# Two stack loads moved behind the band copies in SyncE's step of the first attention

## The chip, the cores and the metric

The kernel runs on one core of one Trainium2 chip. A core has TensorE (PE in the profile, with PEld for its weight loads), VectorE (DVE), ScalarE (ACT), GpSimd (POOL) and SyncE (SP), which work beside each other and wait for each other through semaphores. All DMAs of this program are issued by SyncE, on one queue that 16 DMA engines serve. The metric is the device time of one execution in microseconds (us), lower is better.

## The reference, cut to what matters

The program is a block of two layers on x of 8 x 512 x 128 (batches, positions T, channels C): attention, layer norm, feed-forward, layer norm, and the same again with another attention and another feed-forward. The change touches only the first attention, which has 16 heads of 8 channels and scores with two relative-position terms:

```
rel = arange(t)[None, :] - arange(t)[:, None]
rel_pos = clip(rel + 64, 0, 127);  p2c_pos = clip(-rel + 64, 0, 127)
scores = einsum('bhqd,bhkd->bhqk', Q, K) * scale
c2p = einsum('bhqd,shd->bhqs', Q, pos_key) * scale      # then gathered at rel_pos
p2c = einsum('bhkd,shd->bhks', K, pos_query) * scale    # then gathered at p2c_pos, transposed
probs = softmax(scores + c2p + p2c, axis=-1)
ctx = einsum('bhqk,bhkd->bhqd', probs, V);  out = ctx @ Wo.T + bo
```

## The kernel before

Five stages follow each other: an opening that projects queries, keys and values, the first attention (`attention(0)`), a stage between the layers, the second attention (`attention(1)`) and a dense stage. Both attentions are made by one function; what holds for the first alone stands under `if rel`.

The first attention goes through 128 heads (8 batches by 16), one after the other, in four row tiles of 128 each. One pass is called a step. Each engine has its own list of steps: 4 steps written out (`FIRST`), a hardware loop of 8 steps a turn, and the rest written out. In step n the engines are at different heads:

- PE multiplies score tiles six tiles ahead of head n (`score_tile`), turns the probabilities of head n, weighs the values of the group before (`weigh`), forms the key side of head n+7 (`key_side`, L741) between the turn of tile 1 and that of tile 2, and the correction of head n+5 (`correction`, L748 and L749) at the step's end. Its order is fixed: an instruction that waits holds all behind it.
- DVE puts in the far side of a tile (`mix`, L936), adds the band (`finish`, L948), takes the row maximum (`row_max`, L956) and copies the key side out (`key_out`, L755).
- ACT takes exponentials (L1046), copies turned probabilities (L1053) and, last in its step, the correction of head n+5 (`corr_out`, L761).
- SP, in step n (`sync_step`, L675), issues the DMAs by which position terms are sheared through memory and by which later heads' data come in. "Stack" is the tile `a_stks`, which holds a head's queries and keys, split in bf16 parts.

What SP issues in step n, before the change, in this order:

| piece | line | head | waits for | KB |
|---|---|---|---|---|
| key-side write, `shear_a_write` | L634 | n+6 | DVE copied the key side | 256 |
| two stack loads, `head_load` | L608, L609 | n+8 | PE finished the score tiles of head n | 96 and 48 |
| correction write, `shear_b_write` | L646 | n+4 | DVE added the band of head n, ACT copied the correction | 256 |
| band read, `shear_b_read` | L652 | n+3 | the correction write of head n+3 landed | 512 |
| table and offset loads (every fourth step) | L621, L628, L629 | a group of 4 | nothing | 96 and 48 |
| skewed read, `shear_a_read` | L640 | n+6 | the key-side write of this step landed | 256 |
| group store and values load (every fourth step) | L671, L673 | a group of 4 | ACT copied the group's output | 256 and 72 |

A stack load of head n+8 goes into the slot of head n; PE reads it first in `key_side` of its step n+1. The band read of head n+3 is awaited by DVE before `finish` of that head, also in its step n+1. The skewed read of head n+6 is awaited by PE before `correction` of that head, at the end of its step n+1. The four steps after which a group is complete are called a group here, and its fourth step, which issues the table, offset, store and values DMAs too, the long step.

The two stack loads are these lines:

```
sp.dma_start(stk[j][0:SR, KS:QLO + 1, :], rows).then_inc(stk_in[j], 16)
sp.dma_start(stk[j][0:SR, QHI, :], rows[:, 1, :]).then_inc(stk_in[j], 16)
```

`hold(q, event, value)` makes the queue wait until a semaphore has reached a value, and counts the wait.

Of the kernel before, what the change touches and what calls it, by code (L numbers as in the profile page):

```python
# [50 lines left out]
CORR_AHEAD, KEY_AHEAD, LOAD_AHEAD = 5, 7, 8  # L51
# [13 lines left out]
def build(nc, t):  # L65

    top = ExitStack()
    with top:
# [430 lines left out]
        def attention(layer):  # L499
# [9 lines left out]
            def s(name):  # L509
                return sem(f"a{layer}_{name}")  # L510
# [30 lines left out]
            score_mm, fixed, added, maxed, exped = (s(n) for n in ("score_mm", "fixed", "added", "maxed", "exped"))  # L541
# [53 lines left out]
            def hold(q, event, value):  # L595

                q.wait_ge(event, BASE + value)
                q.sem_inc(held_off, 1)
# [3 lines left out]
            def head_load(sp, h):  # L602

                j, b = h.slot, h.n // H
                own = bass.ts(h.n % H, DH)
                if rel:
                    rows = stack[0][b, :, own].rearrange("a c j t -> (c j) a t")
                    sp.dma_start(stk[j][0:SR, KS:QLO + 1, :], rows).then_inc(stk_in[j], 16)  # L608
                    sp.dma_start(stk[j][0:SR, QHI, :], rows[:, 1, :]).then_inc(stk_in[j], 16)  # L609
                else:  # L610
                    src = stack[1][b, own].rearrange("c j w -> (c j) w")
                    spins = src[:, 3 * T:5 * T + 2].rearrange("r (a t) -> r a t", a=2)[:, :, 0:T]
                    sp.dma_start(stk[j][0:SR, KEY:NEAR + 1, :].rearrange("r a t -> r (a t)"), src[:, 0:3 * T]).then_inc(stk_in[j], 16)
                    sp.dma_start(stk[j][0:SR, FAR, :], src[:, 2 * T:3 * T]).then_inc(stk_in[j], 16)
                    sp.dma_start(stk[j][SR:R1, EDGE, :], src[:, T + 1:2 * T + 1]).then_inc(stk_in[j], 16)
                    sp.dma_start(stk[j][SR:R1, NEAR:FAR + 1, :], spins).then_inc(stk_in[j], 16)

            def tab_load(sp, h):

                src = table[bass.ds(h.n % H, GROUP)].rearrange("h r c -> r h c")  # L620
                sp.dma_start(tabs[0:SR, h.slot:h.slot + GROUP, :], src).then_inc(tab_in[h.slot // GROUP], 16)  # L621

            def offset_load(sp, h):

                src, own = offsets[h.n // H, bass.ds(h.n % H, GROUP)], slice(h.slot, h.slot + GROUP)
                event = offset_in[h.slot // GROUP]
                for arr in (QLO, QHI):
                    sp.dma_start(stks[RA:RB, own, arr, :], src[:, arr - QLO].rearrange("h k t -> k h t")).then_inc(event, 16)  # L628
                sp.dma_start(stks[RB:RS, own, KS, :], src[:, 2:4].rearrange("h a k t -> (a k) h t")).then_inc(event, 16)  # L629

            def shear_a_write(sp, h):

                hold(sp, key_copied, h.n + 1)
                sp.dma_start(shear_a[h.slot % 4, :, SPAN:SPAN + T], keyside[h.slot % 4][:, :]).then_inc(a_written[h.slot % 4], 16)  # L634

            def shear_a_read(sp, h):

                hold(sp, a_written[h.slot % 4], 16 * (h.use(4) + 1))
                skew = bass.AP(shear_a.tensor, (h.slot % 4) * 128 * PITCH_A, [[PITCH_A + 1, 128], [1, T]])
                sp.dma_start(sheared[h.slot % 4][:, :], skew).then_inc(sheared_in[h.slot % 4], 16)  # L640

            def shear_b_write(sp, h):

                hold(sp, corr_copied, h.n + 1)
                dst = shear_b[h.slot % 4, :, REL:PITCH_B].rearrange("p (n c) -> p n c", n=NT)[:, :, 0:REL]
                sp.dma_start(dst, corr[h.slot % 2][:, :, :]).then_inc(b_written[h.slot % 4], 16)  # L646

            def shear_b_read(sp, h):

                hold(sp, b_written[h.slot % 4], 16 * (h.use(4) + 1))  # L650
                skew = bass.AP(shear_b.tensor, (h.slot % 4) * 128 * PITCH_B + REL, [[PITCH_B - 1, 128], [1, NT * wide]])
                sp.dma_start(band[h.slot % bands][:, :, :].rearrange("p n c -> p (n c)"), skew).then_inc(band_in[h.slot % bands], 16)  # L652

            def edge_write(sp, h):

                hold(sp, corr_copied, h.n + 1)
                dst = shear_e[h.slot % E_RING].rearrange("(n p) c -> p n c", p=128)[:, :, REL:2 * REL]
                sp.dma_start(dst, corr[h.slot % corrs][:, :, :]).then_inc(e_written[h.slot % corrs], 16)

            def edge_read(sp, h):  # L660

                hold(sp, e_written[h.slot % corrs], 16 * (h.use(corrs) + 1))
                skew = bass.AP(shear_e.tensor, (h.slot % E_RING) * T * PITCH_E + REL,
                               [[PITCH_E - 1, 128], [128 * PITCH_E, NT], [1, REL]])
                sp.dma_start(band[h.slot % bands][:, :, :], skew).then_inc(band_in[h.slot % bands], 16)

            def group_store(sp, h, more):

                g = h.use(GROUP)
                hold(sp, out_copied, g + 1)  # L670
                sp.dma_start(heads_out[bass.ts(g, GROUP)], outs[:, :]).then_inc(out_written, 16)  # L671
                if more:
                    sp.dma_start(vs[h.slot // GROUP][:, 0:GROUP * NT * VC], values[g + vslots]).then_inc(v_in[h.slot // GROUP], 16)  # L673

            def sync_step(sp, i, j, left, weighed=True):  # L675

                n = unroll * i + j
                if rel:
                    if left >= CORR_AHEAD + 1:
                        shear_a_write(sp, Head(i, j + CORR_AHEAD + 1))  # L680
                    if left >= LOAD_AHEAD:
                        hold(sp, score_mm, 4 * (n + 1))
                        head_load(sp, Head(i, j + LOAD_AHEAD))
                    if left >= CORR_AHEAD - 1:
                        hold(sp, added, 4 * (n + 1))
                        shear_b_write(sp, Head(i, j + CORR_AHEAD - 1))
                    if left >= CORR_AHEAD - 2:
                        shear_b_read(sp, Head(i, j + CORR_AHEAD - 2))
                    if j % GROUP == GROUP - 1 and left >= LOAD_AHEAD + GROUP:
                        tab_load(sp, Head(i, j + LOAD_AHEAD + 1))  # L690
                    if j % GROUP == GROUP - 1 and left >= LOAD_AHEAD:
                        offset_load(sp, Head(i, j + LOAD_AHEAD + 1 - GROUP))
                    if left >= CORR_AHEAD + 1:
                        shear_a_read(sp, Head(i, j + CORR_AHEAD + 1))
                else:
                    if left >= CORR_AHEAD:
                        edge_write(sp, Head(i, j + CORR_AHEAD))
                    if weighed and left >= CORR_AHEAD - 1 or 0 < j < FIRST and not weighed:
                        if weighed:
                            hold(sp, added, 4 * (n + CORR_AHEAD - bands))  # L700
                        edge_read(sp, Head(i, j + CORR_AHEAD - 1))
                    if left >= LOAD_AHEAD:
                        if not isinstance(i, int) or n + LOAD_AHEAD >= unroll:
                            hold(sp, maxed, 4 * (n + LOAD_AHEAD - unroll + 1))
                        head_load(sp, Head(i, j + LOAD_AHEAD))
                if weighed and j % GROUP == GROUP - 1:
                    group_store(sp, Head(i, j + 1 - 2 * GROUP), left >= GROUP * (vslots - 1))
# [1416 lines left out]
```

## Time and profile before

| | us |
|---|---|
| median of 3 runs | 1885.64 (1884.05 to 1885.77) |
| the profiled execution's own time | 1885.77 |
| its span, first to last instruction | 1883.3 |
| PE busy | 1703.0 (90%) |
| DVE busy | 1461.2 (78%) |
| ACT busy | 1448.3 (77%) |

The page of the profile cuts the span into 40 slices of 47.1 us and gives the busy share of each in tenths:

```profile
## 2 busy tenths in 40 slices
PE   4469999999999999868758999999999989999998
DVE  5659999999999999859887999999999872443332
ACT  4449999999999999858888999999999972322222
PEclk9669999999999999989879999999999989999999
DMA  6779999999999999766998777777777751010000
```

The first attention is the stretch of 9s that begins in the third slice and ends in the seventeenth, from about 116 us to 780 us. There PE, DVE, ACT and the DMA engines are all nearly full. The second attention has 7s in the DMA row, and the dense stage at the end hardly uses DMA. Two more parts of the page name what the change moves: the chain that ended last, and the DMAs with the time from issue to landing.

```profile
## 4 chain that ended last, share of the span: by engine, by line
PE 45%; DMA 19%; SPq 10%; issue 10%; DVE 6%; ACT 6%; POOL 0%; DVEq 0%; ACTq 0%; POOLq 0%
DMA shear_a<-a_keyside 13%; PE bank L1936 12%; PE bank L842 11%; PE bank L855 7%; DMA a_band<-shear_e 5%; PE bank L821 4%; DVE a_negmax L956 2%; ACT a_probt L1053 2%; PE bank L823 2%; PE bank L1928 1%; PE bank L1929 1%; PE bank L1957 1%; ACT a_prob L1046 1%; PE bank L741 1%; PE bank L748 1%
...
## 6 DMA issues: line engine op xcount, KB each, us to landing
a_band<-shear_b SPq DMA_DIRECT2D x128, 512.0 KB, 5.5
shear_a<-a_keyside SPq DMA_DIRECT2D x128, 256.0 KB, 4.2
a_sheared<-shear_a SPq DMA_DIRECT2D x128, 256.0 KB, 4.0
shear_b<-a_corr SPq DMA_DIRECT2D x128, 256.0 KB, 3.4
```

### The profile page before, as it was taken

Reading aid. Unit: us, or ns where it says so; the run is one execution under the profiler, and the core shown is the slowest. Engines: PE = TensorE matmul, PEld = TensorE weight load, DVE = VectorE, ACT = ScalarE, POOL = GpSimd, SP = SyncE. Lnnn points to the kernel's source line nnn. Section 1 sums busy time; section 2 is a strip of 40 time slices with the busy share of each in tenths; the row PEclk is TensorE's granted clock in tenths of the full one; section 3 lists DMA queues with packets and bytes.
Section 4 is the critical chain, followed back from the end, with each engine's and each line's share of the span. In section 5 each row is a group of like instructions: output and inputs, shape, how many; then the busy total and the mean of one; then the engine's idle time right before and its main releaser. Section 6 shows DMA issues by size and latency. Waiting matters only on the chain.

```text
span 1883.3 us, 45550 instructions
## 1 busy us (share of the span) xinstructions
PE 1703.0 (90%) x12438; PEld 1047.7 (56%) x12438; DVE 1461.2 (78%) x3533; ACT 1448.3 (77%) x2573; POOL 80.1 (4%) x102
## 2 busy tenths in 40 slices
PE   4469999999999999868758999999999989999998
PEld 2146666666666666545535666666666544455453
DVE  5659999999999999859887999999999872443332
ACT  4449999999999999858888999999999972322222
POOL 0000000000000000015410000000000000000000
PEclk9669999999999999989879999999999989999999
DMA  6779999999999999766998777777777751010000
GB/s 200 275 244 282 291 302 297 295 286 288 279 296 291 286 289 292 239 192 207 350 329 250 218 219 225 220 220 219 221 224 218 219 156 44 28 39 22 22 6 11
DMA packets 414360, 404.45 MB, mean 215 GB/s; under 512 B 36969, under 2 KB 334561, under 8 KB 414177
## 3 DMA queue, kind: packets, MB, share of 16 engines
q1 hardware_dynamic: 414305, 403.80, 69.4%
q8 instruction: 24, 0.39, 0.1%
q14 instruction: 31, 0.25, 0.0%
HBM read 226.89 MB, written 176.30 MB: 214 GB/s over the span
## 4 chain that ended last, share of the span: by engine, by line
PE 45%; DMA 19%; SPq 10%; issue 10%; DVE 6%; ACT 6%; POOL 0%; DVEq 0%; ACTq 0%; POOLq 0%
DMA shear_a<-a_keyside 13%; PE bank L1936 12%; PE bank L842 11%; PE bank L855 7%; DMA a_band<-shear_e 5%; PE bank L821 4%; DVE a_negmax L956 2%; ACT a_probt L1053 2%; PE bank L823 2%; PE bank L1928 1%; PE bank L1929 1%; PE bank L1957 1%; ACT a_prob L1046 1%; PE bank L741 1%; PE bank L748 1%
## 5 line engine op out<-in xcount | busy, mean ns | idle before, releaser
L1046 ACT ACTIVATE a_prob<-bank,a_negmax 128x512 f32<-128x512 f32 x1024 | 697.4, 735 | 50.3 <-DVE a_negmax L956 47.8
L956 DVE TENSOR_REDUCE a_negmax<-bank 128x1 f32<-128x512 f32 x1024 | 698.5, 682 | 0.1
L842 PE MATMUL bank<-ident,a_prob 128*128 128x128 f32 x4096 | 597.6, 279 | 18.9 <-ACT a_probt L1053 15.2
L1053 ACT COPY a_probt<-bank 128x512 f32<-128x512 f32 x1024 | 586.7, 629 | 20.5 <-PE bank L842 20.0
L842 PEld LDWEIGHTS bank<-ident,a_prob 128*128 128x128 f32 x4096 | 446.4, 142 | 85.4 <-issue 49.4
L948 DVE TENSOR_TENSOR bank<-bank,a_band 128x128 f32<-128x128 f32 (+3 forms) x1024 | 349.0, 341 | 56.5 <-DMA a_band<-shear_e 23.0
L821 PE MATMUL bank<-a_stks 74*128 74x192 bf16 (+7 forms) x1024 | 325.3, 318 | 29.3 <-ACT a_prob L1046 25.4
L855 PE MATMUL bank<-a_probt,a_vs 128*32 128x256 f32 (+1 forms) x2792 | 294.6, 495 | 0.4 <-ACT a_probt L1053 0.4
L821 PEld LDWEIGHTS bank<-a_stks 74*128 74x128 bf16 (+1 forms) x1024 | 100.2, 98 | 204.9 <-ACT a_prob L1046 182.3
L823 PE MATMUL bank<-a_stks 74*128 74x320 bf16 (+5 forms) x768 | 201.7, 263 | 0.0
L936 DVE COPY_PREDICATED bank<-a_mask,bank 128x128 f32<-128x128 uint32 (+1 forms) x512 | 139.4, 272 | 27.7 <-PE bank L827 26.6
L2002 DVE TENSOR_TENSOR d_drop<-bank,d_s 128x128 f32<-128x128 f32 x32 | 7.1, 282 | 170.4 <-PE bank L1957 170.4
L748 PE MATMUL bank<-ident,a_sheared 128*128 128x128 f32 x512 | 106.6, 286 | 29.8 <-DMA a_sheared<-shear_a 22.0
L755 DVE COPY a_keyside<-bank 128x512 f32<-128x512 f32 x128 | 87.8, 686 | 39.4 <-PE bank L741 39.2
L827 PE MATMUL bank<-a_stks 74*128 74x128 bf16 (+1 forms) x512 | 109.7, 214 | 7.9 <-DVE bank L936 6.8
L1936 PE MATMUL bank<-d_ha,d_h1T 128*128 128x512 f32 x256 | 112.3, 592 | 0.0
L1936 PE MATMUL bank<-d_hb,d_h2T 128*128 128x512 f32 x256 | 111.2, 592 | 0.0
L761 ACT COPY a_corr<-bank 128x512 f32<-128x512 f32 x128 | 75.9, 593 | 40.2 <-PE bank L749 25.4
L748 PEld LDWEIGHTS bank<-ident,a_sheared 128*128 128x128 f32 x512 | 74.9, 146 | 43.2 <-issue 24.5
L749 PE MATMUL bank<-a_tabs,a_stks 65*128 65x128 bf16 x512 | 98.4, 226 | 0.0
L855 PEld LDWEIGHTS bank<-a_probt,a_vs 128*32 128x32 f32 x2792 | 56.2, 108 | 67.9 <-issue 67.8
L1987 ACT ACTIVATE d_hb<-bank,d_fs 128x512 f32<-128x512 f32 x32 | 22.0, 687 | 90.6 <-PE bank L1936 90.6
(179 smaller groups left out, 1600.5 us busy)
## 6 DMA issues: line engine op xcount, KB each, us to landing
a_band<-shear_b SPq DMA_DIRECT2D x128, 512.0 KB, 5.5
shear_a<-a_keyside SPq DMA_DIRECT2D x128, 256.0 KB, 4.2
a_sheared<-shear_a SPq DMA_DIRECT2D x128, 256.0 KB, 4.0
shear_b<-a_corr SPq DMA_DIRECT2D x128, 256.0 KB, 3.4
shear_e<-a_corr SPq DMA_DIRECT2D x128, 256.0 KB, 2.3
a_band<-shear_e SPq DMA_DIRECT2D x128, 256.0 KB, 3.2
a_stks<-stack SPq DMA_DIRECT2D x256, 96.0 KB, 2.5
a_stks<-stack SPq DMA_DIRECT2D x384, 48.0 KB, 2.4
```

Of the source, the lines that this page charges most:

```text
L748: pe.matmul(corr_bank[:, q], sheared[h.slot % 4][:, q], ident[:, :], is_transpose=True, start=True, stop=False)
L821: last = pe.matmul(score[:, 0:c], k[:, qlo, q], k[:, keys, 0:c], start=True, stop=True)
L823: last = pe.matmul(score[:, c:T], k[:, qhi, q], k[:, keys, c:T], start=True, stop=True)
L827: last = pe.matmul(other[:, 0:e - a], k[:, qhi, q], k[:, keys, a:e], start=True, stop=True)
L842: last = pe.transpose(turned_bank[k][:, n * 128:(n + 1) * 128], prob[h.slot % 2][:, n, k * 128:(k + 1) * 128], ident[:, :])
L855: part = pe.matmul(cbank[32 * j:32 * j + VW, cols], vs[g][:, at:at + VW], probt[h.slot + j][:, k, cols], start=(k == 0), stop=(k == NT - 1 ...
L936: v.copy_predicated(score[:, a:e], mask[:, 0:e - a], other[:, 0:e - a]).then_inc(fixed, 1)
L948: v.tensor_tensor(score[:, a:e], score[:, a:e], band[h.slot % bands][:, n, w:w + e - a], ALU.add).then_inc(added, 1)
L956: v.tensor_reduce(negmax[h.slot % 2][:, n:n + 1], score[:, :], AX.X, ALU.max, negate=True).then_inc(maxed, 1)
L1046: nc.scalar.activation(prob[h.slot % 2][:, n, :], score[:, :], ACT.Exp, bias=negmax[h.slot % 2][:, n:n + 1]).then_inc(exped, 1)
L1053: nc.scalar.copy(probt[h.slot][:, k, :], turned_bank[k][:, :]).then_inc(copied, 1)
L1936: last = pe.matmul(dst[:, :], w[:, k, 128 * m:128 * m + 128], src[:, k, :], start=(k == 0), stop=(k == KH - 1))
```

## The change

In SP's step of the first attention the two stack loads of head n+8 move from behind the key-side write to behind the band read. The wait ahead of them is now for the row maxima of head n instead of its score tiles. Nothing else changes; the other four engines' instructions are the same.

```
                     if left >= CORR_AHEAD + 1:
                         shear_a_write(sp, Head(i, j + CORR_AHEAD + 1))
-                    if left >= LOAD_AHEAD:
-                        hold(sp, score_mm, 4 * (n + 1))
-                        head_load(sp, Head(i, j + LOAD_AHEAD))
                     if left >= CORR_AHEAD - 1:
                         hold(sp, added, 4 * (n + 1))
                         shear_b_write(sp, Head(i, j + CORR_AHEAD - 1))
                     if left >= CORR_AHEAD - 2:
                         shear_b_read(sp, Head(i, j + CORR_AHEAD - 2))
+                    if left >= LOAD_AHEAD:
+                        hold(sp, maxed, 4 * (n + 1))
+                        head_load(sp, Head(i, j + LOAD_AHEAD))
```

On SP's queue an ordinary step of the first attention reads so (L634 key-side write, L608 and L609 stack loads, L646 correction write, L652 band read, L640 skewed read; - is before, + is the change, names carry the buffer's number):

```order
 L634 DMA shear_a<-a_keyside_76 128x512
-L608 DMA a_stks<-stack 48x2x512
-L609 DMA a_stks<-stack 48x512
 L646 DMA shear_b<-a_corr_67 128x4x128
 L652 DMA a_band_68<-shear_b 128x1024
+L608 DMA a_stks<-stack 48x2x512
+L609 DMA a_stks<-stack 48x512
 L640 DMA a_sheared_80<-shear_a 128x512
```

The correction write and the band read now follow the key-side write at once, and the stack loads stand between the band read and the skewed read.

In the long step of a group, on the same queue, the table and offset loads (L621, L628) follow:

```order
 L634 DMA shear_a<-a_keyside_74 128x512
-L608 DMA a_stks<-stack 48x2x512
-L609 DMA a_stks<-stack 48x512
 L646 DMA shear_b<-a_corr_67 128x4x128
 L652 DMA a_band_70<-shear_b 128x1024
+L608 DMA a_stks<-stack 48x2x512
+L609 DMA a_stks<-stack 48x512
 L621 DMA a_tabs<-table 48x4x256
 L628 DMA a_stks<-offsets 3x4x512 x2
```

Here the stack loads stand between the band read and the table load.

## Rows read from the trace of the kernel before

**Rows 1.** The page, part 1: busy us (share of the span) and instructions by engine.

```profile
PE 1703.0 (90%) x12438; PEld 1047.7 (56%) x12438; DVE 1461.2 (78%) x3533; ACT 1448.3 (77%) x2573; POOL 80.1 (4%) x102
```

**Rows 2.** Windows view: stretch, its us, busy us (count) per engine, clock, DMA share.

```profile
200.00:400.00 200.00, 196.53 (x1872) 131.74 (x1871) 189.01 (x487) 189.26 (x346) 0.00 (x0) 1.00 0.94 294
```

**Rows 3.** Waits of SP's queue, 126 to 780 us: in total, times, longest us.

```profile
SPq L598 <- DMA shear_a<-a_keyside: 99.4, 88, 3.6
SPq L598 <- ACT a_corr L761: 11.5, 18, 2.1
SPq L598 <- DVE a_keyside L755: 4.2, 7, 1.1
```

**Rows 4.** Timeline of SP's queue, steps 47 and 48: start us, us.

```profile
372.73 0.32 SPq L634 DMA_DIRECT2D shear_a<-a_keyside  x1
...
375.31 0.39 SPq L646 DMA_DIRECT2D shear_b<-a_corr  x1
375.81 0.44 SPq L652 DMA_DIRECT2D a_band<-shear_b  x1
376.51 0.34 SPq L621 DMA_DIRECT2D a_tabs<-table  x1
...
380.38 0.33 SPq L634 DMA_DIRECT2D shear_a<-a_keyside  x1
...
381.75 0.35 SPq L609 DMA_DIRECT2D a_stks<-stack  x1
382.29 0.39 SPq L646 DMA_DIRECT2D shear_b<-a_corr  x1
382.79 0.44 SPq L652 DMA_DIRECT2D a_band<-shear_b  x1
```

**Rows 5.** DMA view, 375.7 to 376.7 us: count, KB, us to landing.

```profile
a_band<-shear_b SPq DMA_DIRECT2D x1, 512.0 KB, 5.1
...
a_tabs<-table SPq DMA_DIRECT2D x1, 96.0 KB, 4.6
```

**Rows 6.** DMA view, 382.7 to 383.2 us, the band read of step 48.

```profile
a_band<-shear_b SPq DMA_DIRECT2D x1, 512.0 KB, 5.3
```

**Rows 7.** DMA view, 126 to 780 us, medians of the two stack loads.

```profile
a_stks<-stack SPq DMA_DIRECT2D x119, 96.0 KB, 3.0
...
a_stks<-stack SPq DMA_DIRECT2D x119, 48.0 KB, 3.3
```

**Rows 8.** Timeline of PE, key sides of heads 13, 53, 56, 61, 69, 72, 125.

```profile
156.82 0.39 PE L741 MATMUL bank<-a_stks,a_tabs 65*128 65x512 bf16 x1
...
371.40 0.39 PE L741 MATMUL bank<-a_stks,a_tabs 65*128 65x512 bf16 x1
...
387.60 0.39 PE L741 MATMUL bank<-a_stks,a_tabs 65*128 65x512 bf16 x1
...
414.28 0.39 PE L741 MATMUL bank<-a_stks,a_tabs 65*128 65x512 bf16 x1
...
458.14 0.39 PE L741 MATMUL bank<-a_stks,a_tabs 65*128 65x512 bf16 x1
...
474.34 0.39 PE L741 MATMUL bank<-a_stks,a_tabs 65*128 65x512 bf16 x1
...
764.18 0.39 PE L741 MATMUL bank<-a_stks,a_tabs 65*128 65x512 bf16 x1
```

**Rows 9.** Timeline of SP's queue, steps 63 and 64.

```profile
460.00 0.32 SPq L634 DMA_DIRECT2D shear_a<-a_keyside  x1
...
468.10 0.33 SPq L634 DMA_DIRECT2D shear_a<-a_keyside  x1
...
470.51 0.44 SPq L652 DMA_DIRECT2D a_band<-shear_b  x1
```

**Rows 10.** DMA view, 470.4 to 470.8 us, the band read of step 64.

```profile
a_band<-shear_b SPq DMA_DIRECT2D x1, 512.0 KB, 6.4
```

**Rows 11.** DMA view, 361.9 to 362.2 us, the band read of step 44.

```profile
a_band<-shear_b SPq DMA_DIRECT2D x1, 512.0 KB, 3.9
```

More of the change, by code:

```diff
@@ L680, in sync_step @@
                         shear_a_write(sp, Head(i, j + CORR_AHEAD + 1))
-                    if left >= LOAD_AHEAD:
-                        hold(sp, score_mm, 4 * (n + 1))
-                        head_load(sp, Head(i, j + LOAD_AHEAD))
                     if left >= CORR_AHEAD - 1:
@@ L688, in sync_step @@
                         shear_b_read(sp, Head(i, j + CORR_AHEAD - 2))
+                    if left >= LOAD_AHEAD:
+                        hold(sp, maxed, 4 * (n + 1))
+                        head_load(sp, Head(i, j + LOAD_AHEAD))
                     if j % GROUP == GROUP - 1 and left >= LOAD_AHEAD + GROUP:
```

## The prediction, written before the changed kernel ran

> **What bounds the kernel now.** I read the page's busy times first: PE is busy for 90% of the span [rows 1], more than any other engine. The windows view of the stretch in which the change lies, the first attention, is sharper: from 200 to 400 us PE is busy for 196.5 of 200 us at full clock, DVE and ACT for 189, and the DMA share is 0.94 [rows 2]. So PE sets the pace, and whatever makes PE stand still there is lost; but the DMA queue has hardly any room either. Eight heads take 414.28 - 371.40 = 42.88 us on PE, read from the key sides of heads 53 and 61 [rows 8], which is 5.36 a head. From head 13 to head 125 the same rows give 764.18 - 156.82 = 607.4 us for 14 such eights, where 14 x 42.88 would be 600.3. So the whole loop loses only 7 us to anything but its steady pace.
>
> Then the waits of SP's queue in that loop [rows 3]: 99.4 us, in 88 of about 120 steps, for the key-side write to land, 11.5 us for ACT's copy of the correction, and 4.2 us for DVE's copy of the key side. SP is thus a second chain (write, landing, skewed read, next write) that runs at nearly PE's pace with little slack. When a DMA that PE or DVE needs comes late, it is because this chain and the queue behind it are late.
>
> **The change, part by part.** No instruction is added or dropped. PE, DVE, ACT and POOL have the same lists.
>
> The new wait, for the maxima of head n, costs nothing in the loop. The loads now stand behind the correction write, which waits for ACT's copy of head n+4's correction; ACT makes that at the end of its step n-1, behind the exponentials of head n, and these need the maxima. So the maxima are always there first. Behind this wait stand the skewed read and the next key-side write; in the first step alone, whose correction was copied in the opening, it may hold them, once and for no more than one row maximum.
>
> The correction write and the band read go out earlier by up to the issue of two loads. In step 48 the second load starts at 381.75 and the correction write at 382.29, 0.54 later [rows 4], so the two take some 1.1 us. DVE waits for the band read hardly at all, so this can only take away part of the 7 us of loss above: between 0 and 7. I take 5, since a late band read and a late skewed read are what the loss looks like, and both get slack if PE slips for another reason.
>
> The stack loads go back in the queue, behind 256 + 512 KB. This is where the time should change. Now they land 3.0 and 3.3 us after issue [rows 7], long before PE's key side wants them. How long does a small load behind a band read take? The table load is just that: issued at 376.51 behind the band read of 375.81 [rows 4], it lands after 4.6 us, at 381.1, and the band read after 5.1, at 380.9 [rows 5]. So a load behind the band read lands 0.2 us after it. The band read itself then has 144 KB less ahead of it, so the loads should land about when the band read lands today.
>
> The Trainium skill (DMA: Bandwidth & Descriptors, section on queues, rings and completion order) says that each DMA engine takes a queue's descriptors in ring order, but that completion is not first in, first out over the engines. By the first half the loads cannot overtake, and this sum holds; by the second they might finish before the band read, and the sum would shrink towards the second rival below. The table load's landing, 0.2 us behind the band read [rows 5], speaks for the first.
>
> When does PE want them? Step 48 loads head 56, whose key side starts at 387.60 [rows 8]. The band read of step 48 is issued at 382.79 [rows 4] and lands 5.3 us later [rows 6], at 388.1: 0.5 us too late. In step 64 the band read goes at 470.51 [rows 9] and takes 6.4 [rows 10], so 476.9, where head 72's key side starts at 474.34 [rows 8]: 2.5 late. In step 44 the band read takes 3.9 [rows 11], 1.4 less than in step 48, and is not late. Only the step after a long one is late as a rule: the long step takes 380.38 - 372.73 = 7.65 us on SP [rows 4], against 5.36 on PE.
>
> Does PE pay this lateness once or again and again? If SP keeps its own times, PE slips once, and the next late load finds PE already late. But where SP has been waiting for PE (for the key side that DVE copies), SP slips along, and the next group pays again. The least distance from a key side to its write is head 53's, 371.40 [rows 8] to 372.73 [rows 4], 1.33 us. A group's price is its lateness less the distance beyond 1.33 in the long step ahead of it. Step 48: 0.5 - 0 = 0.5. Step 64: head 69's key side at 458.14 [rows 8], its write at 460.00 [rows 9], distance 1.86, so 2.5 - 0.5 = 2.0.
>
> There are 27 groups in the loop from step 12 to step 116. In 16 the band read lands as in steps 44 and 48, late and not late in turn: 8 x 0.5 = 4.0. In 11 it lands like step 64's or between; 5 are as late as step 64, 5 x 2.0 = 10.0, and for the other 6 I take a quarter of that, 6 x 0.5 = 3.0 (between 0 and 12). Together 17.0. Off this comes what the band read gains by its earlier issue where the queue had run dry: between 0 and 1.1 a priced group; I take 0.2, as the loads' own transfer comes back behind it, so 19 x 0.2 = 3.8.
>
> The long step on SP may grow: there the correction's copy is what ended the wait before the correction write in many groups, and the two loads, which were issued during that wait, now come after it, 1.1 us. The correction write to the band read and the loads then keep their times, so I cost it at nothing. Its cover is the skewed read's slack; without it the price is up to 27 x 1.1 = 30 us.
>
> Sum: 17.0 - 3.8 - 5 = +8.2 us, say +8.5 for the half microsecond by which the second load trails the first. On the profiled execution's 1885.77 (span 1883.3 and 2.5 around it) that is 1894.3; the median of the runs, 1885.64, is the same within 0.1.
>
> **The rivals.**
>
> The lateness is paid once. SP mostly waits for its own write to land (99.4 us) and rarely for the key side (4.2 us) [rows 3], so SP may keep its times when PE slips. Then PE slips by the largest lateness and no more, about 2.8 us, and this slack takes part of the 7 us away: 1885.77 + 2.8 less 0 to 3, so 1886 to 1888.6. Against it: in steps 47 and 48 SP had no slack at all towards the key side (1.33).
>
> Faster: the loads do not fall behind the band read, and the band read's earlier issue counts. The place is DVE's wait for the band and PE's wait for the skewed read between 415 and 530 us and after 690 us, where the 7 us are lost. If the loads still land within about 3.3 us of their own issue, as today [rows 7], they are in time even when issued 1.1 to 1.7 us later, and up to 7 us come back: 1879 to 1882. It decides at a load landing of some 5 us. Against it speaks the table load [rows 5].
>
> Much slower: the longer long step is not covered. SP's chain has no room to give 1.1 us in 27 groups, the next key-side writes are late, and PE waits for the corrections: +8.5 and most of 30, 1916. Against it: between the late steps SP has caught up before the next long step, since it waits there for the key side.
>
> **How the numbers follow.** Forecast (price paid again in part of the groups) 0.56, with its own range 1889 to 1903; paid once 0.20; faster 0.16; much slower 0.08. A measurement of this kernel cannot tell less than 0.2%, 3.8 us, from no change. Of the forecast's share about 0.05 lies within it, so: slower 0.51 + 0.08, with 0.01 from paid once, 0.60; same 0.24; faster 0.16. Predicted 1894.3. The range goes from 1882, the upper end of the faster case, to 1908, by which a part of the unpriced 30 us is taken in.
>
> **What would show it.** In the profile after, the stack loads' landing should be 4.5 to 5.5 us in the median in place of 3.0 and 3.3. PE's (or its weight load's) idle time before L741 should be released by the DMA of the stack, in a dozen to two dozen places, mostly in steps right after a long one, worth 10 to 20 us in all; before, no such wait is there. Eight heads should take more than 42.88 us in most eights. DVE's waits for the band and PE's for the skewed read should shrink. SP should wait less for the write's landing and more for the key side's copy. The prediction is wrong if L741 waits for no load, or if the loads land in some 3 us; its mechanism is right but its size wrong if the waits are there and come to under 5 or over 25 us.

## The result, and the profile after

| | us |
|---|---|
| before, median of 4 runs | 1885.7 (1884.05 to 1888.66) |
| changed, median of 4 runs | 1936.22 (1933.13 to 1944.24) |
| ratio | 1.0272, 95% interval 1.0239 to 1.0307 |

The change makes the kernel slower by 50.5 us. 8.5 were forecast, with 1908 as the upper end of the range. The profiled execution of the changed kernel took 1944.98 us, with a span of 1943.2; its page, from parts 1 and 2:

```profile
span 1943.2 us, 45550 instructions
...
PE 1721.4 (89%) x12438; PEld 1057.7 (54%) x12438; DVE 1463.4 (75%) x3533; ACT 1453.5 (75%) x2573; POOL 80.1 (4%) x102
...
PE   5469999999999999977667999999999989999998
DVE  5568888889888888876977899999999973344332
...
PEclk8669999999999999988978999999999989999999
DMA  6778988889888888855999777777777761001000
```

DVE and the DMA engines, at 9 in most slices of the first attention before, are mostly at 8 now: neither has become the limit. PE is busy for 18 us more though it does the same work, which already points at its clock [rows 1]. The DMA view of 126 to 834 us has the medians of the two stack loads, 3.0 and 3.3 us before [rows 7]:

```profile
a_stks<-stack SPq DMA_DIRECT2D x119, 96.0 KB, 3.4
...
a_stks<-stack SPq DMA_DIRECT2D x119, 48.0 KB, 4.3
```

The groups of instructions at the key side, 126 to 834 us (line, engine, what, busy us and mean ns, then idle time before and what ended it):

```profile
L755 DVE COPY a_keyside<-bank 128x512 f32<-128x512 f32 x121 | 83.1, 687 | 62.8 <-PE bank L741 62.6
L741 PE MATMUL bank<-a_stks,a_tabs 65*128 65x512 bf16 x121 | 47.1, 390 | 41.6 <-DMA a_stks<-stack 25.9 <-issue 13.1 <-ACT a_probt L1053 1.9
```

PE now stands for 41.6 us before its key sides, and DVE stands behind it. The trace names a stack load as what ended 25.9 us of this; for the rest it names ACT (1.9) or nothing. The landing times settle it: summed by head over heads 16 to 119, 38.0 us of the idle time stand before heads 0 mod 4, those loaded in the step after the long one, and 0.2 before all others; and before all 26 of these heads the key side starts within 0.25 us of the later load's landing. Two other waits are gone. The kernel before had these between 126 and 780 us, and the changed one has neither between 126 and 834:

```profile
DVE bank L948 <- DMA a_band<-shear_b: 2.3, 4, 0.8
PE bank L748 <- DMA a_sheared<-shear_a: 1.9, 3, 1.1
```

The waits of SP's queue in the same stretch (the changed kernel's answer to [rows 3]):

```profile
SPq L598 <- ACT a_corr L761: 119.4, 75, 3.4
SPq L598 <- DMA shear_a<-a_keyside: 43.5, 33, 2.3
SPq L598 <- DVE a_keyside L755: 2.9, 2, 2.7
```

SP used to wait mostly for its own write to land; now it waits mostly for ACT's copy of the correction, ten times as long as before. One group in detail, the same steps 63 and 64 as in [rows 9]; timeline of SP's queue (start us, us):

```profile
488.36 0.35 SPq L634 DMA_DIRECT2D shear_a<-a_keyside  x1
490.42 0.37 SPq L646 DMA_DIRECT2D shear_b<-a_corr  x1
490.91 0.43 SPq L652 DMA_DIRECT2D a_band<-shear_b  x1
491.81 0.34 SPq L608 DMA_DIRECT2D a_stks<-stack  x1
492.34 0.35 SPq L609 DMA_DIRECT2D a_stks<-stack  x1
492.94 0.32 SPq L621 DMA_DIRECT2D a_tabs<-table  x1
...
494.91 0.35 SPq L640 DMA_DIRECT2D a_sheared<-shear_a  x1
...
496.72 0.33 SPq L634 DMA_DIRECT2D shear_a<-a_keyside  x1
497.35 0.37 SPq L646 DMA_DIRECT2D shear_b<-a_corr  x1
497.84 0.58 SPq L652 DMA_DIRECT2D a_band<-shear_b  x1
498.84 0.34 SPq L608 DMA_DIRECT2D a_stks<-stack  x1
499.37 0.35 SPq L609 DMA_DIRECT2D a_stks<-stack  x1
```

The long step goes from 488.36 to 496.72, 8.36 us, where the same step took 8.10 before [rows 9] and step 47 took 7.65 [rows 4]. Single steps differ, so the means over 25 long steps count: 7.81 us before, 8.51 now. SP stood 1.7 us before the correction write; ACT's copy ended at 490.32. Before, the two loads were issued in that time; now they come behind it. In the means over the 25 steps the correction write keeps its place (2.13 us after the key-side write before, 2.10 now), and from the band read to the next key-side write it takes 5.92 us instead of 5.17. The DMA view of 498.7 to 499.6 us has the landing of step 64's two loads:

```profile
a_stks<-stack SPq DMA_DIRECT2D x1, 96.0 KB, 4.4
a_stks<-stack SPq DMA_DIRECT2D x1, 48.0 KB, 5.3
```

499.37 + 5.3 = 504.7. PE's timeline there (idle time and its releaser in brackets):

```profile
501.58 0.63 PE L842 MATMUL bank<-ident,a_prob 128*128 128x128 f32 x4
502.14 0.64 PE L855 MATMUL bank<-a_probt,a_vs 128*32 128x256 f32 x8
504.77 0.39 PE L741 MATMUL bank<-a_stks,a_tabs 65*128 65x512 bf16 x1 [1.99 <-DMA a_stks<-stack]
```

PE stands 2 us for the load that SP issued last. And then comes what no term of the prediction had. Windows of the same place (PE, PEld, DVE, ACT and POOL busy, granted clock, DMA share, GB/s):

```profile
501.60:506.20 4.60, 2.61 (x30) 1.42 (x28) 2.35 (x8) 2.67 (x6) 0.00 (x0) 1.00 1.03 348
506.20:509.60 3.40, 3.40 (x26) 2.51 (x19) 2.11 (x6) 1.72 (x4) 0.00 (x0) 0.50 0.70 205
```

After a stretch in which PE was busy for 2.61 of 4.60 us the granted clock is 0.50, 1.2 GHz, for 3.4 us, and PE is busy throughout. There are 11 stretches of 3.4 us at 1.2 GHz in the loop, 37.5 us in all; before, the loop had none and ran at 2.4 GHz. The Trainium skill (TensorE: Matmul & The Clock Gate, section on oscillation in real kernels) describes kernels whose stops for a DMA send the array back to half its clock, so that the next piece of work starts slow; this trace agrees in kind.

To compare runs I use one number from each trace beside its ratio: the group time, the mean distance between the key sides of heads 14 and 18, 18 and 22, and so on to 118, 26 groups of four heads. It was 21.67 us before and is 23.59 now: 1.92 x 26 = 50 us. That is not the whole difference of the two traces, whose spans are 59.9 us apart: 4 us more lie in the rest of the loop and 6 behind it. The profiled execution of the changed kernel was also its longest; in the others the granted clock over the span was 0.950 to 0.953, here 0.948. So the shares below are those of this trace.

The 10 groups that touch a half-clock stretch take 24.93 us, the 16 others 22.75. But PE also stood longer in the former, 1.88 us before the key side in the mean against 1.21. Among stops of nearly the same length, 1.50 to 1.78 us, five groups with a half-clock stretch take 24.68 us and three without take 23.22, so the clock costs about 1.5 us each time. A fit over all 26 says the same, and meets every group within 0.1 us: a group takes 21.57 us, plus 0.98 times PE's stop, plus 1.51 where the clock fell. Hence, of the 50 us, PE's stops are some 38 and the clock 15, and about 3 come back elsewhere.

### The profile page after: what moved, and what is told of

It is laid out like the page before. It is cut to its first block, busy times and chain, and to the rows that moved or that the text cites. A ratio compares the mean times of both kernels' runs of the same rounds, so it can differ in the third digit from the quotient of the medians.

```text
span 1943.2 us, 45550 instructions
## 1 busy us (share of the span) xinstructions
PE 1721.4 (89%) x12438; PEld 1057.7 (54%) x12438; DVE 1463.4 (75%) x3533; ACT 1453.5 (75%) x2573; POOL 80.1 (4%) x102
## 4 chain that ended last, share of the span: by engine, by line
PE 43%; SPq 16%; issue 13%; DMA 12%; DVE 8%; ACT 7%; DVEq 0%; POOL 0%; ACTq 0%; POOLq 0%
PE bank L1936 11%; PE bank L842 10%; PE bank L855 6%; DMA a_band<-shear_e 6%; DMA a_stks<-stack 4%; PE bank L821 4%; DVE a_negmax L956 3%; ACT a_probt L1053 3%; ACT a_prob L1046 2%; PE bank L823 2%; PE bank L1928 1%; PE bank L1929 1%; DVE bank L948 1%; PE bank L741 1%; PE bank L748 1%
## 5 line engine op out<-in xcount | busy, mean ns | idle before, releaser
L842 PE MATMUL bank<-ident,a_prob 128*128 128x128 f32 x4096 | 603.8, 281 | 21.8 <-ACT a_probt L1053 15.5
L842 PEld LDWEIGHTS bank<-ident,a_prob 128*128 128x128 f32 x4096 | 451.8, 143 | 89.9 <-issue 51.3
L741 PE MATMUL bank<-a_stks,a_tabs 65*128 65x512 bf16 x128 | 51.3, 400 | 58.1 <-DMA a_stks<-stack 25.9
```

Of the source, the lines that this page charges most:

```text
L842: last = pe.transpose(turned_bank[k][:, n * 128:(n + 1) * 128], prob[h.slot % 2][:, n, k * 128:(k + 1) * 128], ident[:, :])
```

## The experiments

Every run was taken beside the kernel before on its own chip. "Long step" is the mean over the 25 long steps of steps 16 to 115, key-side write to key-side write; "half clock" is the time at clock 0.50 within the loop. Group times, steps and stops come from one trace of each run. A load is called late where PE starts the key side within 0.25 us of the landing of the later of the two loads.

| run | ratio to before, interval | group us | long step us | half clock us |
|---|---|---|---|---|
| before | 1 | 21.67 | 7.81 | 0 |
| the change | 1.0272 (1.0239 to 1.0307) | 23.59 | 8.51 | 37.5 |
| order only | 1.0284 (1.0258 to 1.0309) | 23.48 | 8.53 | 37.5 |
| wait only | 1.0008 (0.9992 to 1.0024) | 21.66 | 7.65 | 0 |
| loads between write and read | 1.0020 (1.0004 to 1.0035) | 21.82 | 7.71 | 0 |
| loads behind the wait alone | 1.0096 (1.0070 to 1.0122) | 22.51 | 8.22 | 3.4 |
| changed after the long step only | 1.0027 (1.0002 to 1.0051) | 21.90 | 7.69 | 0 |
| changed in the three others | 1.0129 (1.0088 to 1.0170) | 22.80 | 8.51 | 0 |
| changed in the long step only | 1.0111 (1.0069 to 1.0153) | 22.30 | 8.10 | 0 |
| changed in the three short ones | 1.0044 (1.0026 to 1.0061) | 21.92 | 7.33 | 0 |
| change, key side later | 1.0188 (1.0139 to 1.0236) | 22.81 | 8.43 | 3.4 |
| old order, key side later | 1.0102 (1.0059 to 1.0146) | 22.34 | 7.35 | 0 |
| change, store from ACT | 1.0065 (1.0038 to 1.0091) | 22.39 | 7.21 | 0 |
| old order, store from ACT | 1.0035 (1.0017 to 1.0054) | 22.17 | 6.31 | 0 |
| change, filler on PE | 1.0220 (1.0179 to 1.0260) | 23.04 | 8.47 | 0 |
| old order, store early | 1.0023 (0.9999 to 1.0048) | 21.74 | 7.70 | 0 |

**Order only.** The change with the old wait.

```
-                        hold(sp, maxed, 4 * (n + 1))
+                        hold(sp, score_mm, 4 * (n + 1))
```

> The new order of SP's queue with the old wait (score tiles of head n) ahead of the two stack loads. Theory A (the loads land too late for PE's key side, because they stand last, behind the correction's wait, the correction write and the band read): the same as the change, ratio to before 1.022 to 1.030, heads 0 mod 4 with loads landing within 0.25 us of their key side. Theory C (the new wait for the row maxima costs): 1.00 to 1.005.

1938.09 us, the same as the change. The order is the whole of it.

**Wait only.** The old order with the new wait.

```
-                        hold(sp, score_mm, 4 * (n + 1))
+                        hold(sp, maxed, 4 * (n + 1))
```

> The old order with the new wait (row maxima of head n in place of its score tiles). The maxima come after the key side's copy on DVE, by a COPY_PREDICATED and a TENSOR_REDUCE, about 1 us, so SP may stand up to 0.6 us in steps where it had no slack. Theory A: ratio 1.000 to 1.006, loads landing well ahead of the key side (slack 2 us and more). Theory C: 1.02 or more.

1885.81 us. The wait costs nothing that can be told, even in the place where it could be last. Theory C is out.

**Loads between write and read.** `head_load` (with its wait) stands between `shear_b_write` and `shear_b_read`.

```
                         shear_b_write(sp, Head(i, j + CORR_AHEAD - 1))
+                    if left >= LOAD_AHEAD:
+                        hold(sp, maxed, 4 * (n + 1))
+                        head_load(sp, Head(i, j + LOAD_AHEAD))
                     if left >= CORR_AHEAD - 2:
                         shear_b_read(sp, Head(i, j + CORR_AHEAD - 2))
```

> Loads (with the new wait) behind the correction write, ahead of the band read. They still stand behind ACT's correction copy but not behind the 512 KB. Theory A in its queue form (the band read ahead of them is what makes them late): they land 1.5 to 2.5 us earlier than in the change, the lateness of about 1.5 us a group is mostly gone, ratio 1.000 to 1.008. Theory B (standing behind the wait for ACT's correction copy, which closes a loop through PE, is what costs): 1.018 to 1.027.

1889.19 us. Ahead of the 512 KB instead of behind them the loads land 5.0 us into the step after the long one (mean), where in the change it is 7.3, and almost all of the loss is gone. So being behind ACT's copy is not enough for the loss, against theory B.

This run also shows something that the others hide. SP issues the same things behind ACT's wait as in the change, and yet the long step does not grow (7.71 us): the copy comes 1.29 us after the key-side write, where it comes at 1.82 before and at 2.00 in the change, and the skewed read goes out at 5.70 us, before at 5.77. So issues behind the wait did not lengthen the step here: ACT's copy came sooner by about as much.

**Loads behind the wait alone.** The wait for ACT's copy is made first, then the loads, then the write.

```
+                    if left >= CORR_AHEAD - 1:
+                        hold(sp, corr_copied, n + CORR_AHEAD)
+                    if left >= LOAD_AHEAD:
+                        hold(sp, maxed, 4 * (n + 1))
+                        head_load(sp, Head(i, j + LOAD_AHEAD))
                     if left >= CORR_AHEAD - 1:
```

> Loads behind the waits of the correction write but ahead of both the write and the band read: only the wait is ahead of them, no other transfer. Theory A in its queue form: 0.998 to 1.004, slack of the loads at the key side over 1.5 us. Theory B: 1.018 to 1.027, since the wait ahead of them is that of the change. If both parts count, the ratio rises from this run over the one with the loads between to the change.

1904.5 us: slower than with the loads between write and read. Neither theory had that. No load is late here; what is late are the reads. The waits in this run, 126 to 780 us:

```profile
PE bank L750 <- DMA a_sheared<-shear_a: 19.9, 24, 1.8
DVE bank L950 <- DMA a_band<-shear_b: 11.7, 20, 1.5
```

In the long step the correction write goes out 1.7 us after ACT's copy, 0.1 in the change; the step grows to 8.22 us, and DVE and PE stand for the band and for the skewed read. This was the first run to show that the length of SP's long step can go with a loss without any late load.

**Changed after the long step only, and in the three others.** The same `if`, by the step's place in its group.

```
+ loads last where j % GROUP == 0, in the old place elsewhere      (first run)
+ loads last where j % GROUP != 0, in the old place elsewhere      (second run)
```

> The change only in every fourth step, the one after the long step; in the other three the stack loads and their wait stand as before. Before, in this step, the band read lands 7.7 us after the step's first issue and the key side starts 6.5 us after it, so the loads come 1.2 us late if they land with the band read; the long step keeps its 7.8 us. Theory D (late loads in this one step, paid by every group): ratio 1.006 to 1.018, loads of heads 0 mod 4 landing at the key side in most groups. Theory E (the long step, grown by two issues behind ACT's wait, is what costs): 0.999 to 1.004.

> The complement: the change in three steps of four, the long one among them, and the old order in the step after the long one. The loads there are early again; the long step is longer by up to 1.1 us. Theory D: 1.000 to 1.008. Theory E: 1.015 to 1.027. If the two parts stand in series on one path (the long step, then the late loads), this run and the one with the change in the fourth step alone cost clearly less together than the whole change's 51 us.

1896.3 us (beside 1891.35 for before) and 1917.12 us. In the first 24 of 106 loads are late and PE stands 10.1 us for them, and yet it costs only 0.3%, 6 us over the 26 groups: the long step keeps its length. The lower bound of 1.006 was missed, so theory D alone falls. In the second no load after the long step is late, and it costs 1.3%. That is over theory D's range and under theory E's, and the run is not clean: 49 of its 106 loads are late, for heads 1 to 3 mod 4, PE stands 15.1 us before these key sides, and in other places for the skewed read (15.9 us). Together the two runs cost 1.6%, not 2.7%: the two parts make something that neither has.

**Changed in the long step only, and in the three short ones.** The cleaner pair, by the long step itself.

```
+ loads last where j % GROUP == GROUP - 1      (first run)
+ loads last where j % GROUP != GROUP - 1      (second run)
```

> The change in the long step alone (every fourth); the other three steps keep the old order. Theory G (the growth of SP's long step behind ACT's correction copy costs about 1 us a group by itself): SP's long step 8.3 to 8.6 us against 7.8, no load late at the key side, no half clock, ratio 1.009 to 1.015. If the long step's growth were harmless by itself and only the loads' place counted: 0.999 to 1.004.

> The complement: the change in the three other steps, the old order in the long one. Theory G: the long step keeps 7.8 us; the loads of the step after it come late but SP keeps its times, so the lateness is paid about once; ratio 1.001 to 1.007, no half clock or hardly any. If the late loads are what the change costs: 1.012 or more.

1906.71 and 1895.24 us (before: 1889.01). The long step alone costs 1.1%, the short ones 0.4%, both ratios as theory G had them. Its details were not all right. In the first run the long step went to 8.10 us, less than expected, and loads are late after all, 21 of 106: those that the long step itself issues, for which PE stands 8.6 us. In the second the long step fell to 7.33 us, and PE stands 10.4 us at the key side, where it is 38.0 in the change with the same loads late. The waits of the first run, 126 to 780 us:

```profile
PE bank L751 <- DMA a_sheared<-shear_a: 8.8, 14, 1.6
PE bank L744 <- DMA a_stks<-stack: 7.0, 12, 0.9
DVE bank L951 <- DMA a_band<-shear_b: 4.3, 8, 1.1
```

Three of the DMAs behind ACT's wait are late by turns, so this run does not tell the length of the step from the late loads in it. And again the pair adds up to 1.55%, 1.2% short of the whole.

**Change, filler on PE.** Nine transposes of the identity ahead of the key side that stands for a late load; they write the bank that the key side then overwrites.

```
+                        if (j + KEY_AHEAD) % GROUP == 0:
+                            for f in range(FILL):          # FILL = 9
+                                pe.transpose(key_bank[:, 128 * (f % NT):128 * (f % NT) + 128], ident[:, :], ident[:, :])
                         key_side(pe, Head(i, j + KEY_AHEAD), key_bank)
```

> The changed order, with 9 extra transposes of the identity (about 0.12 us each, 1 us a group) put on PE ahead of its key side in the one step of four where it stands about 1.5 us for the loads. They write the key side's bank, which the key side then overwrites. Theory H (in the change, the clock's fall to its lower level after these stops costs about 22 us on top of the long step): the half-clock stretches of the loop, 34 us in the change, go to under 10, and the kernel gets faster than the change by 10 to 22 us in spite of 27 us more work on PE: ratio to before 1.014 to 1.022. If the clock costs nothing of its own: 1.027 or more.

1927.8 us. Timeline of PE in one group, and the windows view of the loop in this run:

```profile
498.93 0.64 PE L856 MATMUL bank<-a_probt,a_vs 128*32 128x256 f32 x8
499.50 1.20 PE L882 MATMUL bank<-ident 128*128 128x128 f32 x9
500.54 0.38 PE L742 MATMUL bank<-a_stks,a_tabs 65*128 65x512 bf16 x1
...
126.00:790.00 664.00, 639.00 (x5985) 435.99 (x5984) 584.58 (x1502) 588.76 (x1068) 0.00 (x0) 1.00 0.89 273
```

The clock stays at 1.00 through the loop, the long step is as long as in the change, and with about a microsecond of added work a group the group time falls from 23.59 to 23.04, which is 14 us over 26 groups. In the profiled executions the way from head 13's key side to head 125's is 645.2 us, in the change 660.8. The ratio, 1.0220, is at the edge of what was expected; it is 0.5%, some 10 us, under the change's, and the two intervals overlap a little. By the clock rows the added work removed every half-clock stretch of the loop; by the group times that is worth about what the comparison of groups gave for the clock, 15 us.

**Key side later, in both orders.** On PE behind the next score tile and turn, on DVE behind the next mix and maximum.

```
-                    if left >= KEY_AHEAD: ... key_side(...)
                     score_ahead_of(pe, i, j, left, 2)
                     turn(pe, own, 2)
+                    if left >= KEY_AHEAD: ... key_side(...)
```

> The changed order, with PE's key side moved behind the next score tile and turn (some 0.9 us later in PE's step) and DVE's copy of it behind the next tile's mix and maximum. Theory D and its clock part (PE stands at the key side for the loads, long enough that the granted clock drops to half for 3.4 us every second group): each group gives back about 0.9 us and most of the half-clock time goes, ratio 1.006 to 1.016. If PE's stop at the key side were only a symptom of a late SP chain, it stays at 1.024 or more.

> Control: the same later key side with the old order of SP's queue, where the loads had 2.8 us in hand. Every theory: 0.998 to 1.005; what it costs is to be taken off the run with the changed order.

1927.93 and 1910.71 us. The control costs 1.0% by itself, more than expected. The changed order on top of it costs 0.9%, not 2.7%, the idle time before the late key sides falls from 38 to 10 us, and one half-clock stretch is left of 11. The ratio itself, 1.0188, lies above the 1.016 expected, since the control costs what was not foreseen. The clock rows fit the filler run by another way: with less of a stop there, the half-clock stretches go.

**Store from ACT, in both orders.** `group_store` (store and values load, every fourth step) leaves SP and is issued from ACT's queue behind the third exponential.

```
+                        if weighed and j % GROUP == GROUP - 1:
+                            group_store(act, Head(i, j + 1 - 2 * GROUP), left >= GROUP * (vslots - 1))
                         copy_turned(act, own, 3)
```

> The changed order, with the group's store and the values load (two DMAs in every fourth step, 1.1 us of SP's long step) issued from ACT's queue behind the third exponential of the same step. Theory F (SP's long step is on the path ahead of the late loads): SP's long step falls from 8.5 to about 7.4 us, each group gives back 0.7 to 1.1 us and the half-clock time goes with the stalls; ACT pays 0.7 us of issue a group. Ratio 1.005 to 1.017. If only the place of the loads counts and not the long step: 1.023 to 1.03.

> Control and candidate: the same two DMAs from ACT's queue with the old order. SP's long step, 7.8 us before, gets shorter than 7; the 7 us that the loop lost to late reads may come back. 0.996 to 1.002; over 1.003 if ACT's issue time is not hidden.

1901.16 and 1895.67 us. With the long step at 7.21 us the changed order costs 5.5 us more than the old one beside it, not 51. PE's stops before the key sides of heads 16 to 119, 38.2 us in the change, are 4.2 us. This is the strongest single run for the cause: the loads are as far back in the queue as in the change, and ACT's copy and the skewed read stand where they do there in the long step (1.98 and 6.49 us after the key-side write, 2.00 and 6.51 in the change); only the two issues behind them are gone, and the next step begins earlier. The control costs 0.35%, as was expected if ACT's issues are not hidden; that they are the reason is not shown.

**Old order, store early.** The store and values load stand ahead of `shear_a_read` in the long step.

> The old order, with the group's store and values load moved ahead of the skewed read in the long step, so that they are issued while SP waits for its write to land instead of after it. Theory G says a shorter long step gives back part of the 7 us that the loop lost before: 0.995 to 1.000 if SP's long step falls below 7.3 us. But the store waits for ACT's copy of the group, which may come later than the write's landing; then the skewed read is late and it costs: 1.000 to 1.01.

1891.86 us, no difference that can be told. The long step only fell to 7.70 us, since the store waits for ACT's copy; SP stood 9.1 us for it between 130 and 760 us. No run beat the kernel before.

## Why the prediction was wrong

**What bounds the kernel.** Right: PE, busy for 196.5 of 200 us, with SP's chain close behind. The chain was named as a second limit, and then its lengthening was not priced.

**The wait.** Right: nothing.

**The band read goes out earlier.** Right in kind: DVE's wait for the band and PE's for the skewed read are gone. Of the 5 us some 3 are seen, as the difference between 21.67 us, a group before, and the 21.57 that the fit leaves without stop and clock. This rests on the fit; no run isolates it.

**The loads land with the band read.** Right in kind, forecast too late in size: 3.4 and 4.3 us in the median where 4.5 to 5.5 were forecast, 5.3 for the second load in the step shown. PE stands at the key side for them, in the step after the long one, as forecast, but for 38 us in place of 10 to 20. By the prediction's own sign, over 25 us, this is the right wait with the wrong size.

**The price of the lateness.** For what it covered, nearly right: with the old order in the long step PE stands 10.4 us at the key side, and the run costs 0.24 x 26 = 6 us by the group times, 0.4% or 8 us by the ratio, where the whole sum, which left the long step out, was 8.5. Its terms (17.0, less 3.8, less 5) were not measured one by one. It is more than the 2.8 us of the rival "paid once".

**The long step, "so I cost it at nothing".** This is the step that failed. It was argued that the correction write, the band read and the loads keep their times, and the skewed read has slack. They did keep them: the correction write stands at 2.13 us before and 2.10 now. But behind the loads SP issues seven more DMAs in the long step and then the next key-side write, and it had only some 0.4 us of idle time to give there, before the skewed read. So the skewed read moved from 5.77 to 6.51 us after the key-side write, and the next step began 0.70 us later, 8.51 in place of 7.81. The loads of the step after it came later with it, and PE's stop for them grew. What this is worth is seen from both sides: with the old order in the long step (7.33 us long there), PE's stops are 10.4 us, not 38.0; with two issues taken out of it, the changed order costs 5.5 us more than the old one beside it. Changed alone, the long step costs 0.62 x 26 = 16 us (by the ratio, 1.0111, 21 us), of which PE's stops for its own late loads are a part. The bound of 30 us that stood beside the term was the better number, and the rival built on it was given too little with 0.08: in step 47 SP leaves ACT's wait at 375.31 and issues until 380.38 [rows 4]. That rival had PE waiting for the corrections; it waits for the loads.

**The clock, in no term.** The two parts together put PE's idle time in one place, 1.5 us in the mean before one key side in four. In 10 of the 26 groups the clock then fell, at 1.5 x 10 = 15 us, by groups with stops of the same length. The filler run shows this to be a cost of its own and gives 14 us by the group times, 10 by the ratios.

So the 50 us are: short steps 6, long step 16, clock 15, and 13 more that only the two parts together have. The first two come from runs, the clock from comparing groups, and the 13 are what is left. A loop would explain them, in which PE, once late, makes ACT's copy late, and SP stands for that (119.4 us) with the loads behind it. This is argued, not shown; with the loads between write and read the copy comes sooner and the loop does not close, and why it does so there was not tested. SP did not wait more for the key side, as the prediction had said it would (2.9 us, before 4.2).

## What to carry to other kernels

When an issue is moved from ahead of a wait to behind it, its issue time can be added to the path behind the wait, and everything that the queue issues afterwards moves with it: price the longest step of the queue, not the mean one. It is a bound, not a certainty: here the long step grew in two orders with the loads behind the wait (8.51 and 8.22 us, from 7.81), and not in a third (7.71). A small load put behind a large read landed with it or a little after here (7.91 us into the long step where the read landed at 7.39, and 7.33 where it landed at 6.82 in the step behind). And ask of a new stall where it falls: in the change 38 us stood in 26 places and the clock fell 11 times; in the run changed in the three others 15 us stood before more key sides in shorter stops, and it never fell.

## What was not expected of the hardware

TensorE's clock fell from 2.4 to 1.2 GHz after short stops: each of the 11 stretches begins 0.3 to 1.9 us after a key side before which PE had stood 1.5 to 2.3 us. But not each such stop did it: in four groups of the same trace PE stood 1.6 to 2.1 us and the clock stayed. Filling the stop with 1.2 us of useless transposes in one step of four kept the clock up and made the changed kernel faster by the group times, 23.04 us in place of 23.59.
